# Decoder feed-forward: rounding of the up values and fills of the diagonal buffer on GpSimd, every second sigmoid block rounded on ScalarE

## The reference

```python
def act_qdq(x):                       # one scale for the whole tensor
    scale = max(max(abs(x)) / 32767, 1e-12)
    return clip(round(x / scale), -32768, 32767) * scale
def fixed_qdq_u16(x):
    return clip(round(x * 65536), 0, 65535) / 65536
x    = act_qdq(x)
up   = act_qdq(x @ lpbq_dequant(w_up).T)      # 384 wide
gate = act_qdq(x @ lpbq_dequant(w_gate).T)    # 384 wide
sig  = fixed_qdq_u16(sigmoid(gate))
gate = act_qdq(gate * sig)
o    = act_qdq(gate * up)
return o @ lpbq_dequant(w_down).T
```

## Time and profile before

| | us |
|---|---|
| median of three runs | 2159.82 |
| profiled execution | 2161.72 |
| its span | 2159.9 |
| PE / DVE / ACT / POOL busy in the span | 1994.5 / 1573.6 / 1356.3 / 1017.4 |

### The profile page before, as it was taken

The page is one execution under the profiler, slowest core; times in us unless marked ns, Lnnn a source line. Parts: engine busy times, 40 slices in busy tenths (PEclk is TensorE's granted clock), DMA queues, the critical chain, the costliest instruction groups (busy, mean ns, idle before and its releaser), DMA issues.

```text
span 2159.9 us, 44602 instructions
## 1 busy us (share of the span) xinstructions
PE 1994.5 (92%) x14787; PEld 1694.7 (78%) x14849; DVE 1573.6 (73%) x3446; ACT 1356.3 (63%) x3147; POOL 1017.4 (47%) x1222
## 2 busy tenths in 40 slices
PE   6999989999999999998039999999899999999998
PEld 4787789999999999994037888877677777777776
DVE  4666668888888888777775666666777777787775
ACT  3666656666666666666774666787655555555554
POOL 2555444444444444420003655554356666566665
PEclk7999999999999999998568999999899999999999
DMA  6433400000000000000004443455233333333332
GB/s 174 124 117 117 119 1 1 2 1 2 1 1 2 2 1 2 1 1 1 0 0 132 118 118 113 122 164 156 80 116 120 121 126 119 118 123 122 120 125 97
DMA packets 138907, 161.03 MB, mean 75 GB/s; under 512 B 15340, under 2 KB 99244, under 8 KB 138284
## 3 DMA queue, kind: packets, MB, share of 16 engines
q1 hardware_dynamic: 132524, 153.46, 23.7%
q10 hardware_dynamic: 6160, 4.78, 0.7%
HBM read 119.75 MB, written 38.70 MB: 73 GB/s over the span
## 4 chain that ended last, share of the span: by engine, by line
PE 66%; issue 9%; POOL 8%; DVE 6%; ACT 6%; SPq 3%; DMA 1%; ACTq 1%; POOLq 0%; DVEq 0%
PE bank L947 8%; POOL h_lo L2130 7%; PE bank L273 5%; PE bank L911 5%; PE bank L913 5%; PE bank L912 5%; PE bank L1785 5%; PE bank L958 5%; PE bank L1787 5%; PE bank L1786 5%; PE bank L284 3%; PE bank L255 3%; PE bank L1688 2%; PE bank L254 2%; PE bank L293 1%
## 5 line engine op out<-in xcount | busy, mean ns | idle before, releaser
L2130 POOL TENSOR_TENSOR h_lo<-h,h_hi 128x512 fp32r<-128x512 f32 x264 | 341.5, 1294 | 245.6 <-ACT h_hi L1911 245.5
L1312 POOL TENSOR_TENSOR pw<-ew,rw 128x410 f32<-128x410 f32 x256 | 225.9, 882 | 368.3 <-DVE rw L1171 360.0
L556 DVE TENSOR_REDUCE nmx<-bank 128x4 fp32r<-128x512 f32 (+1 forms) x384 | 238.2, 621 | 209.5 <-PE bank L255 206.8
L1904 ACT ACTIVATE sl<-bank 128x512 f32<-128x512 f32 x264 | 158.0, 598 | 238.6 <-PE bank L1787 237.2
L449 ACT ACTIVATE pt<-bank 128x512 f32<-128x512 f32 (+1 forms) x384 | 229.1, 600 | 124.9 <-PE bank L273 124.0
L1067 ACT ACTIVATE ew<-bank,nmax 128x205 f32<-128x205 f32 x512 | 217.3, 432 | 132.6 <-DVE nmax L1163 132.6
L2049 DVE TENSOR_TENSOR bank<-bank,sl 128x512 f32<-128x512 f32 x264 | 184.2, 698 | 142.6 <-PE bank L1787 114.5
L706 POOL TENSOR_SCALAR_AFFINE_SELECT pt<-pt 128x512 f32<-128x512 f32 x256 | 162.9, 637 | 191.7 <-ACT pt L449 191.6
L273 PE MATMUL bank<-q_pack,k_diag 128*128 128x128 f32 (+1 forms) x1536 | 238.5, 280 | 2.4 <-ACT pt L449 2.1
L273 PEld LDWEIGHTS bank<-q_pack,k_diag 128*128 128x128 f32 (+1 forms) x1536 | 189.6, 181 | 49.1 <-issue 38.7
L947 PE MATMUL bank<-kvt,qs 128*128 128x205 f32 x1024 | 221.2, 339 | 0.0
(11 more groups left out here) (346 smaller groups left out, 5217.1 us busy)
## 6 DMA issues: line engine op xcount, KB each, us to landing
share_b<-share_rows SPq DMA_DIRECT2D x256, 256.0 KB, 3.1
q_rows<-q_hi SPq DMA_DIRECT2D x96, 128.0 KB, 2.7
q_pack<-q_rows SPq DMA_DIRECT2D x32, 384.0 KB
raw<-in_experts SPq DMA_DIRECT2D x33, 192.0 KB, 3.3
q_rows<-q_lo SPq DMA_DIRECT2D x48, 128.0 KB, 2.7
k_diag<-k_rows SPq DMA_DIRECT2D x64, 96.0 KB
q_pack<-q_rows SPq DMA_DIRECT2D x31, 192.0 KB
k_diag<-k_rows SPq DMA_DIRECT2D x124, 48.0 KB
```

The source lines that it names most:

```text
L556: nc.vector.tensor_reduce(m.nmx[:, b % 2, :, 0, c], m.score[c % 2][:, 0:HC * a.columns].rearrange("p (h k) -> p h k", h=HC)[:, :, 0:a.keys ...
L1312: nc.gpsimd.tensor_tensor(m.pw[:, k, :, 0:KW], m.ew[:, k, :, :], m.rw[:, k, :].unsqueeze(2).broadcast_to([128, 2, KW]), ALU.mult)\
L2130: nc.gpsimd.tensor_tensor(m.h_lo[:, k % 3, :], m.h[:, (k + u) % 2, :], m.h_hi[:, k % 3, :].bitcast(F32), ALU.subtract).then_inc(s.los, 1)
```

## The change

The rounding of the up values leaves ScalarE. GpSimd does it, all 8 blocks, in two instructions each: scale and add a large constant (`MAGIC`) in place, then subtract it into int16, with a wait on its own semaphore in between. They stand between the third and the fourth all-reduce. The 16 fills leave ScalarE too and stand on GpSimd between the fourth and the fifth all-reduce. ScalarE rounds the sigmoid of the odd blocks, VectorE only that of the even ones; each has its own semaphore.

```diff
-        self.rounded_sigmoids = sem(f"{stage}_rounded_sigmoids")
+        self.rounded_sigmoids = [sem(f"{stage}_rounded_sigmoids{k}") for k in range(2)]
+        self.up_sums = sem(f"{stage}_up_sums")
...
     def round_sigmoid(n):                     # VectorE
         dve.wait_ge(s.sigmoids, n + 1)
         nc.vector.tensor_scalar(m.u16[:, n % 2, :], m.sig[:, n % 2, :], 65536.0, None, ALU.mult)\
-            .then_inc(s.rounded_sigmoids, 1)
+            .then_inc(s.rounded_sigmoids[0], 1)
     def gated(n):
-        dve.wait_ge(s.rounded_sigmoids, n + 1)
+        dve.wait_ge(s.rounded_sigmoids[n % 2], n // 2 + 1)
...
     for n in range(G):
-        round_sigmoid(n)
+        if n % 2 == 0:
+            round_sigmoid(n)
...
     def sigmoid(n):                           # ScalarE
         act.wait_ge(s.gates, n + 1)
-        wait(act, s.rounded_sigmoids, n - 1)
+        wait(act, s.rounded_sigmoids[n % 2], n // 2)
...
-    def round_up(n):
-        nc.scalar.activation(block(m.up16, n), block(m.up, n), ACT.Identity, scale=col(FU)).then_inc(s.ups, 1)
+    def round_sigmoid(n):
+        act.wait_ge(s.sigmoids, n + 1)
+        wait(act, s.products, n - 1)
+        nc.scalar.activation(m.u16[:, n % 2, :], m.sig[:, n % 2, :], ACT.Identity, scale=65536.0)\
+            .then_inc(s.rounded_sigmoids[1], 1)
...
         sigmoid(n)
-        if n == 1:
-            act.wait_ge(s.scaled, 2)
         if n % 2 == 1:
-            round_up(n // 2)
+            round_sigmoid(n)
     act.wait_ge(s.scaled, 3)
-    diagonals = ...
-    def fill(n): ...                          # nc.scalar.copy
-    act.wait_ge(s.ups, G // 2)
     for n in range(G):
         rounding_sum(n, F2)
-        if n < G // 2:
-            round_up(G // 2 + n)
-        fill(n)
-    act.wait_ge(s.ups, G)
-    for n in range(G):
-        last = fill(G + n)
-    last.then_inc(m.s.zeros, 1)
...
 def ffn_pool(pool, nc, m, s):
-    for n in range(5):
+    def all_max(n):
         pool.wait_ge(s.local_max, n + 1)
         nc.gpsimd.partition_all_reduce(m.gmax[:, n:n + 1], m.lmax[:, n:n + 1], 128,
                                        bass.bass_isa.ReduceOp.max).then_inc(s.all_max, 1)
+    def round_up(n):
+        up = block(m.up, n)
+        nc.gpsimd.tensor_scalar(up, up, m.scal[:, FU:FU + 1], MAGIC, ALU.mult, ALU.add).then_inc(s.up_sums, 1)
+        pool.wait_ge(s.up_sums, n + 1)
+        nc.gpsimd.tensor_scalar(block(m.up16, n), up, MAGIC, None, ALU.subtract).then_inc(s.ups, 1)
+    diagonals = m.k_diag1[:].rearrange("p u h c t -> p (u h c) t")
+    def fill(n):
+        return nc.gpsimd.tensor_copy(diagonals[:, RING * n:RING * n + RING, :],
+                                     m.blocks[:, RING * n:RING * n + RING].unsqueeze(2).broadcast_to([128, RING, 2 * T]))
+    for n in range(3):
+        all_max(n)
+    pool.wait_ge(s.scaled, 2)
+    for n in range(G):
+        round_up(n)
+    all_max(3)
+    pool.wait_ge(s.ups, G)
+    for n in range(2 * G):
+        last = fill(n)
+    last.then_inc(m.s.zeros, 1)
+    all_max(4)
```

## The result

The changed kernel takes 2184.41 us (median of 4 runs, 2183.46 to 2185.05); beside it the kernel before took 2160.2. The ratio is 1.0114, with a 95% interval of 1.0092 to 1.0137: slower by 24.2 us, where 12.2 (2172.0 against 2159.8) was forecast. The profiled execution took 2184.68, its span 2182.9.

A forecast was written before the change was run, and what follows sets the result against it. VectorE was taken to bound the gate stage, ScalarE the first hidden blocks. A fourth all-reduce 12.5 us late, less 3.4 saved, plus 3.3 given back, made 12.4 more: 2172 on the median (2174 profiled), range 2161 to 2188.

The forecast's parts named there:

- the stretch at half clock: Gate and hidden stages, 1032.0 to 1106.3: TensorE idle at half clock, so time on VectorE, ScalarE or GpSimd counts fully.
- both exchanges: GpSimd changes code between all-reduces and roundings, in and out: 6 us each, the first hidden, the second delaying the fourth all-reduce.
- the queue order: On GpSimd the fourth all-reduce stands behind all sixteen roundings, so it comes at 1085.2 instead of 1072.72, 12.5 late.
- rival C: GpSimd's rounding arithmetic costs more than the select: 2186.5 at 2.5 us each, 2203 at 3.53; chance 0.17.
- Roundings of 2.3 and more alone: Sign of being wrong: GpSimd's roundings taking this many us with nothing beside them, instead of near 1.6.
- The step that failed: GpSimd's ups roundings in the gate stage: each of sixteen instructions priced like the select at 1.6 us, 25.6 together.
- The port: GpSimd and VectorE exclude each other except beside maxima; GpSimd waits for seven products and three roundings, 14.2 us.
- The start at 11.82: GpSimd started on time after the program's first configuration pair at 6.4, suggesting an exchange under 5.4 us.
- rival B: The port counts but the code exchange is absent or under 3 us, so VectorE's waits decide: 2167; chance 0.19.
- The gate stage alone: Saving on VectorE and ScalarE from splitting the sigmoid's roundings, without GpSimd's costs: 1.9 us.
- The hidden stage alone: Saving once ScalarE has only rounding sums and VectorE sets the pace, without GpSimd's costs: 3.4 us.
- The fills: Sixteen fills of 0.8 us on GpSimd in the hidden stage hold products by about 0.75, giving back 3.3 us.

The follow-up runs named there:

- e3: Changed kernel with the scaled sigmoids left unrounded as float32 in PSUM, in three pieces a block, so products fetch one operand less from SBUF; 2178.5 us, ratio 1.0102.
- f1: Changed kernel with each subtraction on GpSimd written as times 1.0 plus the constant's negative; 2165.7 us, ratio 1.0019.
- e1: Changed kernel with the fourth all-reduce replaced by a copy of each partition's own maximum, so no second code exchange there; 2171.6 us, ratio 1.0059.
- m1: Small separate program timing GpSimd's instruction forms on 1536 elements, alone and beside VectorE, against no kernel; scale-and-add 1.55 us, subtraction 4.08.
- e6: Kernel before with only the odd sigmoid blocks' rounding moved to ScalarE, five ups roundings behind the last sigmoid; 2156.2 us, ratio 0.9988.
- e8: Kernel before with odd sigmoids rounded on ScalarE, whose hidden stage runs four sums, three ups, four sums, then all sixteen fills; 2148.2 us, ratio 0.9954.
- e9: e8 with six fills on GpSimd timed beside maxima, the sigmoid table loaded early and the first instructions reordered; 2150.9 us, ratio 0.9958.

## Why the prediction was off by half

The sign, the places and the mechanism were right: the stretch at half clock, both exchanges, the queue order that puts the fourth all-reduce behind the last rounding, VectorE idle behind its last gate maximum. The time lies inside the range, and it is near rival C's ("2186.5" at an average of 2.5 an instruction), which had 0.17. C named the right cause and its sign, VectorE idle for ten us (9.89), but that its number is so near is in part luck: the average came out at 2.8, and C's own rule gives 2191 for that. "Roundings of 2.3 and more alone" was on my list of signs of being wrong, and for half of the instructions it came.

**The step that failed** is "The select, one input and some arithmetic, takes 0.637 for 512 ... It is the nearest kind, and I take 1.6", used for all sixteen instructions. It was right for eight, the scale-and-adds: 1.55 alone, and 1.53 to 1.55 in e3, where nothing holds them. For the other eight, the subtractions, it was 4.08: above even the 3.53 that I had taken as the upper bound from the two-input subtraction. Until the last rounding's end, counted from the third all-reduce:

| term | forecast | changed kernel |
|---|---|---|
| start of the first rounding | 6.4 | 7.4 |
| scale-and-adds, own time | 8 x 1.6 = 12.8 | 8 x 1.55 = 12.4 |
| subtractions, own time | 8 x 1.6 = 12.8 | 8 x 4.08 = 32.6 |
| GpSimd waits at the port | 14.2 | 7.8 |
| gaps | 0.8 | 0.7 |
| sum | 47.0 | 60.9 |

The subtraction alone is 19.8 too small, and the port 6.4 too large; behind the last rounding the second exchange is as forecast, and the fills 1.0 cheaper. So the two stages were to take 86.5 and take 99.20. f1 puts the price of the form right and nothing else: 82.24, 8.1 over before, and 2165.7. With the form at its forecast price, the rest of my sum would have been some 4 too high, not too low.

**The port** was taken the right way and shared out wrongly. I let GpSimd wait for seven products and three roundings. With subtractions of 4.08 the products do most of the waiting, seven times 2.9, and that costs nothing, since VectorE has 9.9 to spare at the end; GpSimd waits 7.8 in all (the scale-and-adds' 20.2 of rows less 8 x 1.55: 0.6 four times, 1.4 three times, 1.1 once). In f1, with short instructions, it waits about 12 (36.1 of rows less 16 x 1.5). e3 gives the port's price in the changed kernel by itself, 7.7, which agrees. (The 1.41 in f1's expectation took a wait to end with the product's row.) SBUF — State Buffer of the Trainium skill (Who interferes with whom) says that a VectorE instruction with two SBUF inputs contends with a GpSimd instruction that reads SBUF; that whoever issues first holds the shared pair for the whole instruction it says of VectorE's two-port modes. The contention agrees. For how long a product is held, the rows say: the product of 1040.24 ended at 1044.90, so if its own 1.75 is unchanged it began at 1043.15, 1.0 before the subtraction's row ends.

**The exchanges**, taken as 6 from bounds of 0 and 12.8, are 7.03 and 5.87 by the trace, and e1 takes out 6.0. The start at 11.82, which spoke against them, was misleading. It was a program's first change of code, and in m1 the first one cost at most 0.33 where the later ones cost 5.66 to 6.82; I had allowed for that ("may find its code already there") and still gave the start some weight in rival B. That the same holds for the start at 11.82 is likely, but no run shows it.

**The gate stage alone**: 1.9 forecast, 2.19 in e6 to e8. **The hidden stage alone**: 3.4 forecast, 33.59 - 30.22 = 3.37 in e8. **The fills**: 3.3 forecast, 32.50 - 30.22 = 2.3 (against e8's stage, whose order on ScalarE is another); a held product loses 0.5 rather than 0.75. So the saving that the change was able to give, 5.3 by the forecast, is 5.6, and e8 has all of it with nothing on GpSimd.

The GPSIMD Engine Reference of the Trainium skill (section 3.1) gives 768 ns for 512 elements of a tight loop, which it calls the best case. Neither form is there: the scale-and-add took 0.69, less than that best case, and the subtraction 1.49. Its figure of about 6 us for a first call of freshly loaded code (section 2.1) agrees with the 5.7 to 7.2 measured, but here it came again at every change between all-reduce and arithmetic.

## What to carry to other kernels

When work moves to an engine on which the trace of before shows no instruction of that very form, measure the form by itself first: two instructions that differ in one operation differed here by a factor of 2.8, and the nearest row in the trace fitted only one of them. A move of arithmetic to GpSimd between two all-reduces also cost a change of its code on the way in and another on the way out, and the second one, 5.9 us, stood on the path. And before moving work off an engine, put its queue in the order in which others wait for it: that, with half of a rounding moved to ScalarE, gave the whole saving here.

## What the runs showed of the hardware

- GpSimd's tensor-with-scalar over 1536 elements: 1.47 to 1.55 for the pairs of multiply and add tried, 4.08 to 4.17 for a lone subtraction, addition or multiplication, 5.38 to 5.39 for a subtraction paired with a multiplication. In the forms tried the output type changed nothing, and a column's value in place of a constant cost 0.1 at most. Why isn't known.
- Changing GpSimd's code between arithmetic and all-reduce takes 5.7 to 7.2 us of silence with no row of its own, only a pair of configuration instructions. The first such pair of a program cost at most 0.33 (m1). A copy behind arithmetic (e1), and copies behind an all-reduce, need none.
- A maximum on VectorE and GpSimd's copies or arithmetic run beside each other at full speed (m1: three scale-and-adds in 4.60, the maxima at 1.75; e9: fills of 0.82 and maxima of 1.75).
- A product waiting for a subtraction of 4.08 starts about 1.0 before the end of that row; behind an instruction of 1.47 it was 0.15 (1040.73 + 2.88 - 1.75 in f1, against 1042.00). Both are worked out with a product's own 1.75. What GpSimd does in the rest was not tried.
